# Attention and a routed feed-forward on one core: the down projection in three fp32r passes, the weight splitting begun earlier, the first expert tile turned ahead of the gates

## The chip, the cores and the metric

One core of one Trainium2 chip runs the whole program. The metric is the device time of one execution in microseconds (us), the median of several runs. Engines are called PE (TensorE; PEld its weight loads), DVE (VectorE), ACT (ScalarE), POOL (GpSimd) and SP (SyncE, which here only issues DMAs, in the order of its program). L1034 is line 1034 of the kernel before.

## The reference

The input x is 8 x 1024 tokens of 256 numbers. The steps are these, all in float32:

```python
xn = layernorm(x)
q, k, v = xn @ Wq + bq, xn @ Wk + bk, xn @ Wv + bv      # 4 heads of 256
scores  = (qr . kr + qi . ki) / 16     # of the 4 heads of one token with each other
s       = softmax(scores) @ v, heads swapped, @ Wo + bo
gates   = sinkhorn((xn @ router_w.T + router_b) / temp)  # 3 rounds, 8 experts
top 2 gates of each token, normalised
all_out = (relu(xn @ wg[e]) * (xn @ wp[e])) @ wo[e]      # 256 -> 512 -> 256, expert e
ffn     = xn + sum over the 2 experts of gate * all_out
out     = x + s * silu(ffn)
```

## The kernel before

The kernel goes through these stages.

**Prologue.** SP loads x in 16 blocks of 512 tokens. DVE and ACT normalise it, PE turns it and multiplies it by the router's weights (lines 798 and 808), and SP stores the normalised x to `xn_d`. Beside it the gate and up weights of the 8 experts, 16 pieces of 128 x 1024, are loaded over parts of x that are no longer needed (`load_raw`, line 288), split on POOL into a rounded fp32r part and the rest (`halve`, lines 516 and 519), and both parts are stored to a scratch tensor `w_d` (`store_split`, line 295). The staging buffers are `WH` and `WL`, four pieces deep; the semaphores `s_wst` tell that the stores have landed. When the last stores have landed, DVE splits Wq and Wk into the same buffers (`split`, lines 1132 and 1133). PE folds Wv and Wo into one matrix M (lines 880 and 883, 18 steps), and the first Sinkhorn rounds run between these steps.

**Attention, first half.** `segment(0, QE)` treats the blocks q = 0 to 3. For each there are 24 steps c: with c under 16 a chunk of q or k in three fp32r passes (high by high, high by low, low by high; L952), moved out of PSUM by ACT (L702) and DVE (L1447); with c from 16 on the values (L963), moved by ACT into `UN`, which holds three, and stored by SP (`write_u`, L331). Then 4 score steps follow (L909) with a softmax on DVE. Other DVE work is placed behind certain steps (`side`): the rest of Sinkhorn, the top two, `ranks`. POOL builds one-hot lists (`marks`), and SP stores M to `m_d` before the first block (L325).

**Expert stage.** NM = 135 tiles of 128 gathered tokens. Per tile m, PE runs in this order: `gt(m+1)` (2 transposes, L999), `up(m)` (12 fp32r matmuls of 512 columns with the split gate and up weights, L1017), `ht(m-1)` (4 transposes of the hidden tile, L1026), `down(m-2)` (4 plain fp32 matmuls of 256 columns, L1034; each leaves two records in the trace). ACT moves the turned tokens (`gt`), the relu of the gate, the turned hidden tile (`ht`, L746) and the result (`ye`). DVE subtracts the rounded tokens from the exact ones (`xgl`, L1495) and multiplies relu by up (L1506). POOL gathers tokens and scatters results by indirect DMA. Three experts' weights lie in SBUF; `load_expert` fetches 4096 columns from `w_d` and 1024 from `wo`. Ahead of the stage PE turns the gates into each token's order (`weigh`, 16 matmuls, L939), DVE copies them (`GP`), and only then does `gt(0)` run.

**Attention, second half, and the end.** `segment(QE, NQ)` does the blocks 4 to 15, with the sums over experts, silu and the output beside it.

Of the kernel before, what the change touches and what calls it, by code (L numbers as in the profile page):

```python
# [5 lines left out]
F32 = mybir.dt.float32  # L6
F32R = mybir.dt.float32r
# [29 lines left out]
def program(nc, x, phase, Wq, bq, Wk, bk, Wv, bv, Wo, bo, rw, rb, temp, wg, wp, wo, out):  # L37
# [8 lines left out]
    with ctx:  # L46
# [8 lines left out]
        w_d = nc.dram_tensor("w_d", [E * 128, 4096], F32).ap()  # L55
# [28 lines left out]
        TM = sb("TM", [128, 512])  # L84
        AB = sb("AB", [128, 2, 512])
# [12 lines left out]
        HT = AB[:, :, :].rearrange("p a (c n) -> p a c n", c=4)  # L98
# [96 lines left out]
        s_wst = [sem(f"s_wst{i}") for i in range(4)]  # L195
        s_xb, s_xt, s_xtc, s_xtd = sem("s_xb"), sem("s_xt"), sem("s_xtc"), sem("s_xtd")
# [36 lines left out]
        def raw(i):  # L233

            q = i + 1 if i < 2 * E - 1 else 5
            return WM[:, 1024 * q:1024 * q + 1024], s_x[q], 64 if i < 2 * E - 1 else 80
# [4 lines left out]
        def place_e(x):  # L241

            return 16384 - 5120 * (x % 3)
# [29 lines left out]
        def _(e):  # L273
            for q in range(NQ):
                e.dma_start(X[:, 4 * q:4 * q + 4, :], blk(xf, q)).then_inc(s_x[q], 16)
                if q == 3:
                    e.dma_start(Wv_s, Wv.rearrange("(k p) n -> p k n", p=128)).then_inc(s_wv, 16)
            for j in range(2):
                e.dma_start(Wo_s[j], Wo[512 * j:512 * j + 512, :].rearrange("(c p) n -> p c n", p=128)).then_inc(s_wo, 16)

            def load_raw(i):
                r, s, _ = raw(i)
                if i < 2 * E - 1:
                    e.wait_ge(s_x[i + 1], 48)
                    e.wait_ge(s_rt, 2 * i + 4)
                else:
                    e.wait_ge(s_wlo, 5)
# [3 lines left out]
            def store_split(i):  # L291
# [5 lines left out]
                if i < 4:  # L297
                    w, k = i // 2, i % 2
# [26 lines left out]
            e.dma_start(m_d, WM[:, 16384:24576]).then_inc(s_md, 16)  # L325
# [1206 lines left out]
```

## Time and profile before

| | us |
|---|---|
| median of 3 runs | 1757.52 (1756.17 to 1758.42) |
| the profiled execution's own time | 1760.04 |
| its span, first to last instruction | 1758.1 |
| expert stage, about | 386 to 1084 |
| first attention step | 136.01 |

PE is busy for 96% of the span, and most of the chain of work that ended last is on it. The times of a row are counted from the start of the span. The stage borders are read off the timeline, by the first L952 and the first L1017.

### The profile page before, as it was taken

The numbers are of one execution on the slowest core, as the hardware profiler recorded it, in microseconds if no ns is written. First come the engines' busy times: TensorE is split into PE (matmuls) and PEld (weight loads), VectorE is DVE, ScalarE is ACT, GpSimd is POOL, SyncE is SP. The second block draws the span as 40 slices with busy tenths as digits, with TensorE's granted clock in tenths as the row PEclk, the third lists the DMA queues.
The fourth block names the chain that finished last, engine by engine and source line by source line (L and its number), as shares of the span: only waits on it lengthen the run. The fifth ranks groups of instructions, "written<-read, shape, count | busy, mean of one in ns | idle before, by whom it ended". The sixth has DMA issues, their size and how long they took to land.

```text
span 1758.1 us, 26690 instructions
## 1 busy us (share of the span) xinstructions
PE 1683.1 (96%) x8788; PEld 1280.2 (73%) x8788; DVE 974.2 (55%) x1760; ACT 793.5 (45%) x1207; POOL 744.7 (42%) x865
## 2 busy tenths in 40 slices
PE   5889899999999999999999999999999999999994
PEld 2436766778888888888888888766877767877673
DVE  6567889962222222222222223778777788777785
ACT  4657335513333333333333335367564665644661
POOL 1671178713343333333343433343634645343435
PEclk9989899989999999999999999999999999999997
DMA  9984132172223131313111412424556345554234
GB/s 325 389 341 152 55 120 73 66 258 75 83 80 111 52 111 54 109 55 110 53 52 52 147 52 90 156 97 150 175 180 203 109 156 176 171 180 164 89 120 132
DMA packets 157085, 234.05 MB, mean 133 GB/s; under 512 B 13480, under 2 KB 120800, under 8 KB 155808
## 3 DMA queue, kind: packets, MB, share of 16 engines
q1 hardware_dynamic: 143488, 196.79, 32.7%
q0 software_dynamic: 12960, 35.41, 6.1%
q8 instruction: 81, 1.33, 0.3%
q14 instruction: 44, 0.36, 0.1%
q10 hardware_dynamic: 512, 0.16, 0.0%
HBM read 141.19 MB, written 91.11 MB: 132 GB/s over the span
## 4 chain that ended last, share of the span: by engine, by line
PE 83%; DVE 8%; DMA 3%; SPq 2%; ACT 2%; POOL 1%; issue 1%; ACTq 0%; POOLq 0%; DVEq 0%
PE ps L1017 21%; PE ps L952 17%; PE ps L1034 13%; PE ps L909 11%; PE ps L963 10%; PE ps L1026 3%; DMA WM<-in_L_ffn_wo_dram 2%; PE ps L921 2%; DVE WM L1447 2%; PE ps L999 2%; PE ps L808 1%; DVE UN L1097 1%; ACT WM L702 1%; PE ps L798 1%; DVE US L1381 1%
## 5 line engine op out<-in xcount | busy, mean ns | idle before, releaser
L1017 PE MATMUL ps<-WR,FR 128*128 x1620 | 407.5, 400 | 1.3 <-issue 0.7
L1017 PEld LDWEIGHTS ps<-WR,FR 128*128 128x128 f32 x1620 | 295.9, 189 | 58.7 <-issue 2.2
L702 ACT ACTIVATE WM<-ps,bcs,trig 128x512 f32<-128x512 f32 x256 | 314.0, 1261 | 35.2 <-PE ps L952 20.0
L1447 DVE TENSOR_SCALAR WM<-ps,vec,trig 128x512 f32<-128x512 f32 x256 | 290.1, 1186 | 35.6 <-ACT WM L702 34.8
L546 POOL DMA_INDIRECT y_d<-AUX x135 | 133.7, 990 | 390.6 <-ACT AUX L752 390.6
L1506 DVE TENSOR_TENSOR AUX<-AUX,ps 128x512 f32<-128x512 f32 x135 | 92.9, 688 | 340.6 <-ACT AUX L740 340.6
L1034 PE MATMUL ps<-WM,AB 128*128 x1080 | 255.5, 379 | 0.0
L909 PEld LDWEIGHTS ps<-WM 128*128 128x128 f32 x2048 | 232.2, 193 | 10.5 <-issue 5.8
L909 PE MATMUL ps<-WM 128*128 128x128 f32 x2048 | 236.3, 277 | 3.4 <-DVE TM L1343 3.4
L963 PE MATMUL ps<-WM,XTJ 128*128 128x512 f32 x512 | 237.2, 600 | 0.1
L740 ACT ACTIVATE AUX<-ps 128x512 f32<-128x512 f32 x135 | 80.6, 597 | 316.0 <-PE ps L1017 299.5
L952 PE MATMUL ps<-XH,WH 128*128 128x512 f32 x512 | 205.6, 402 | 4.7 <-issue 3.8
L1034 PEld LDWEIGHTS ps<-WM,AB 128*128 128x128 f32 x1080 | 194.7, 190 | 20.9
L952 PE MATMUL ps<-XH,WL 128*128 128x512 f32 x512 | 200.6, 392 | 0.0
L952 PE MATMUL ps<-XL,WH 128*128 128x512 f32 x512 | 200.6, 392 | 0.0
L1495 DVE TENSOR_TENSOR FR<-ps,FR 128x256 fp32r<-128x256 f32 x135 | 57.3, 425 | 205.3 <-ACT FR L733 205.2
L542 POOL DMA_INDIRECT AUX<-xn_d,AUX x135 | 132.0, 978 | 81.4 <-issue 40.1
L963 PEld LDWEIGHTS ps<-WM,XTJ 128*128 128x128 f32 x512 | 91.6, 190 | 96.9 <-issue 91.8
L558 POOL TENSOR_TENSOR AUX<-AUX,GP 128x256 f32<-128x256 f32 x120 | 77.3, 680 | 162.5 <-DMA AUX<-in_L_attn_x_dram 159.5
L709 ACT ACTIVATE UN<-ps 128x512 f32<-128x512 f32 x128 | 76.3, 596 | 133.6 <-PE ps L963 133.4
L719 ACT ACTIVATE SE<-SS 128x16 f32<-128x16 f32 x64 | 13.8, 216 | 236.6 <-DVE SS L1349 236.5
L752 ACT ACTIVATE AUX<-ps 128x256 f32<-128x256 f32 x135 | 52.0, 385 | 145.9 <-PE ps L1034 145.9
(225 smaller groups left out, 2081.5 us busy)
## 6 DMA issues: line engine op xcount, KB each, us to landing
u_d<-UN SPq DMA_DIRECT2D x128, 256.0 KB, 2.0
US<-u_d SPq DMA_DIRECT2D x64, 512.0 KB, 4.8
WR<-w_d SPq DMA_DIRECT2D x8, 2048.0 KB
AUX<-y_d SPq DMA_DIRECT2D x30, 512.0 KB, 5.8
WM<-in_L_attn_x_dram SPq DMA_DIRECT2D x16, 512.0 KB, 9.4
xn_d<-WM SPq DMA_DIRECT2D x32, 256.0 KB, 6.3
w_d<-WH SPq DMA_DIRECT2D x16, 512.0 KB, 6.4
w_d<-WL SPq DMA_DIRECT2D x16, 512.0 KB, 7.0
```

Source lines behind the costliest of these rows:

```text
L542: e.indirect_dma_start(XG[:, m % 2, :], None, xn_d, bass.IndirectOffsetOnAxis(gidx[:, m:m + 1], 0)).then_inc(s_g[m % 2], 16)
L546: e.indirect_dma_start(y_d, bass.IndirectOffsetOnAxis(toks[:, m - 5:m - 4], 0), YS[:, (m - 5) % 2, :], None).then_inc(s_y[(m - 5) % 2], 16)
L558: ins = e.tensor_tensor(y[:, i, :], y[:, i, :], GP[:, i, k, q, None].broadcast_to([128, D]), ALU.mult)
L702: e.activation(QT[:, 2 * x, i % 2, :].rearrange("p (t h) -> p t h", h=H)[:, :, i // 2], b, ACT.Identity, bias=bcs[:, x, 0, i:i + 1], scale ...
L740: e.activation(GR[:, :], mG[m % 2][:, :], ACT.Relu).then_inc(s_gr, 1)
L909: mm = e.matmul(pS[n % 2][:, 128 * c:128 * c + 128], QT[:, x, h, col:col + 128], QT[:, 2 + x, h, col:col + 128], start=(x == h == 0), stop ...
L952: mm = e.matmul(b[:, :], w[:, k, 128 * c:128 * c + 128], xx[:, k, :], start=(k == 0 and w is WH and xx is XH), stop=(k == 1 and w is WL))
L963: mm = e.matmul(b[:, :], XTJ[:, k, a // 2, :], M_s[:, k, 512 * a:512 * a + 512], start=(k == 0), stop=(k == 1))
L1017: mm = e.matmul(b[:, :], x, WR[:, bass.ds(off[m] + (2048 * z + 1024 * a + 512 * k), 512)], start=(k == 0 and x is xh and z == 0), stop=(k ...
L1034: mm = e.matmul(mY[m % 2][:, 0:256], HT[:, m % 2, c, :], WM[:, bass.ds(off[m] + (4096 + 256 * c), 256)], start=(c == 0), stop=(c == 3))
L1447: e.tensor_scalar(QT[:, 2 * x + 1, i % 2, :].rearrange("p (t h) -> p t h", h=H)[:, :, i // 2], ps[bank(24 * q + c)][:, :], bqk[:, x, i:i + ...
L1506: e.tensor_tensor(HS[:, m % 2, :], GR[:, :], mP[m % 2][:, :], ALU.mult).then_inc(s_h, 1)
```

## The change

**Down projection.** `wo` is split too, in 16 halves of 128 x 512. POOL does this after `xtj(0)` (`halve_down`: a copy that rounds, a subtraction, 128 x 512 each), in two buffers that take turns. SP loads each half (256 KB), waits for the split (`s_ho`), stores both parts (512 KB) to `w_d`, which grows to 6144 columns, and loads the next half but one. Eleven of these `store_half` steps stand ahead of the first `write_u` of block 0, the other five between its first `write_u`s. `ranks` on DVE and `load_expert` wait for these stores. The store of M to `m_d` moves behind block 1's first loads. `down` becomes 12 fp32r matmuls of 256 columns. The turned hidden tile is rounded by ACT into `HTH`; DVE gets a subtraction per tile, `htl`, 128 x 512 out of PSUM, behind its multiplication; the next `ht` waits for it (`s_htl`) instead of for ACT. An expert's load is one DMA of 6144 columns.

**Splitting of gate and up.** Five pieces have buffers of their own (three in `US`, two beyond Wv), and are loaded between x's blocks 1 to 6; the other eleven follow over x as before, from the fourth block stored on. `store_split` begins after the second block stored instead of after the fifth round of splits. The load of Wv moves behind x. ACT waits for five splits before it fills `WvT`.

**Gates.** `weigh` goes out of the segment; PE now does `gt(0)` first, then `weigh`, and DVE copies the gates after `xgl(0)`.

```diff
-            for q in range(NQ + 5):
+            for q in range(NQ):
+                e.dma_start(X[:, 4 * q:4 * q + 4, :], blk(xf, q)).then_inc(s_x[q], 16)
+                if 1 <= q <= 5:
+                    load_raw(q - 1)
...
+            for q in range(NQ + 1):
...
-                if 3 <= q < 3 + 2 * E:
-                    load_raw(q - 3)
-                if q >= 5:
-                    store_split(q - 5)
+                if 3 <= q < 2 * E - 2:
+                    load_raw(q + 2)
+                if q >= 1:
+                    store_split(q - 1)
...
+            def store_half(i):
+                e.wait_ge(s_ho, i + 1)
+                d = w_d[64 * (i - i % 2):64 * (i - i % 2) + 128, 4096:6144].rearrange("p (z f) -> p z f", z=2)
+                e.dma_start(d[:, :, 512 * (i % 2):512 * (i % 2) + 512],
+                            part[i % 2][1].bitcast(F32)).then_inc(s_hs[i % 2], 16)
+                if i + 2 < 2 * E:
+                    load_half(i + 2)
...
+                    if q == 0:
+                        load_half(0)
+                        load_half(1)
+                        for i in range(2 * E - 5):
+                            store_half(i)
+                    if q == 1:
+                        e.dma_start(m_d, WM[:, 16384:24576]).then_inc(s_md, 16)
                     for c in range(8):
                         write_u(q, c)
+                        if q == 0 and c < 5:
+                            store_half(2 * E - 5 + c)
...
+            def halve_down(i):
+                r, hl = part[i % 2]
+                e.wait_ge(s_hr[i % 2], 16 * (i // 2 + 1))
+                if i >= 2:
+                    e.wait_ge(s_hs[i % 2], 16 * (i // 2))
+                ch(e.tensor_copy(hl[:, 0, :], r))
+                e.tensor_tensor(hl[:, 1, :], r, hl[:, 0, :].bitcast(F32), ALU.subtract).then_inc(s_ho, 1)
...
                 for c in range(4):
-                    mm = e.matmul(mY[m % 2][:, 0:256], HT[:, m % 2, c, :],
-                                  WM[:, bass.ds(off[m] + (4096 + 256 * c), 256)], start=(c == 0), stop=(c == 3))
+                    hh, hl = HTH[:, m % 2, c, :], HTL[:, m % 2, c, :]
+                    for x, z in ((hh, 0), (hh, 1), (hl, 0)):
+                        mm = e.matmul(mY[m % 2][:, 0:256], x, WR[:, bass.ds(off[m] + (4096 + 1024 * z + 256 * c), 256)],
+                                      start=(c == 0 and x is hh and z == 0), stop=(c == 3 and x is hl))
...
+            e.wait_ge(s_sm1, 4 * QE - 1)
+            gt(0)
+            weigh()
             e.wait_ge(s_sm1, 4 * QE)
             e.wait_ge(s_gp, 2)
             e.wait_ge(s_ca, 24 * QE)
-            gt(0)
...
             xgl(0)
+            e.wait_ge(s_gp, 1)
+            e.tensor_copy(GP[:, :, :, :].rearrange("p i k q -> p (i k q)"), pD[:, 0:128]).then_inc(s_gp, 1)
...
+                if m >= 1:
+                    htl(m - 1)
+            htl(NM - 1)
```

## Rows read from the trace of the kernel before

**Rows 1.** The page, part 1: busy time of each engine over the span.

```profile
PE 1683.1 (96%) x8788; PEld 1280.2 (73%) x8788; DVE 974.2 (55%) x1760; ACT 793.5 (45%) x1207; POOL 744.7 (42%) x865
```

**Rows 2.** Chain of work that ended last, one expert tile (start, us, what).

```profile
1002.54 2.76 PE ps L1017 x12
1005.30 0.44 PE ps L1026 x4
1005.74 1.73 PE ps L1034 x8
1007.46 0.22 PE ps L999 x2
```

**Rows 3.** Windows view: stretch, engines busy (instructions), granted clock, DMA share, GB/s.

```profile
1000.00:1030.00 30.00, 30.00 (x154) 25.40 (x153) 6.68 (x12) 10.48 (x24) 10.96 (x12) 1.00 0.15 49
```

**Rows 4.** The page, part 5: DVE's product of relu and up, 128 x 512.

```profile
L1506 DVE TENSOR_TENSOR AUX<-AUX,ps 128x512 f32<-128x512 f32 x135 | 92.9, 688 | 340.6 <-ACT AUX L740 340.6
```

**Rows 5.** The same chain: 32 records of fp32 scores; 96 fp32r matmuls of 512 columns.

```profile
254.62 3.64 PE ps L909 x32
...
1083.97 21.86 PE ps L952 x96
```

**Rows 6.** Groups of instructions by form, PE's weight loads: busy us, mean ns, idle before.

```profile
L1017 PEld LDWEIGHTS ps<-WR,FR 128*128 128x128 f32 x1620 | 295.9, 189 | 58.7 <-issue 2.2
L909 PEld LDWEIGHTS ps<-WM 128*128 128x128 f32 x2048 | 232.2, 193 | 10.5 <-issue 5.8 <-DVE TM L1343 3.8 <-ACT UN L709 0.8
```

**Rows 7.** Timeline of POOL: first piece's rounding and subtraction, the last piece's subtraction.

```profile
41.87 1.18 POOL L516 CAST WH<-WM 128x512 fp32r<-128x512 f32 x2 [38.17 <-DMA WM<-in_L_ffn_wg_dram]
43.13 2.50 POOL L519 TENSOR_TENSOR WL<-WM,WH 128x512 fp32r<-128x512 f32 x2
...
122.18 2.94 POOL L519 TENSOR_TENSOR WL<-WM,WH 128x512 fp32r<-128x512 f32 x2
```

**Rows 8.** Windows of 5 us in the prologue, columns as in rows 3.

```profile
15.00:20.00 5.00, 1.24 (x5) 0.85 (x6) 4.46 (x19) 1.85 (x5) 0.00 (x0) 1.00 1.10 348
...
115.00:120.00 5.00, 2.09 (x5) 0.57 (x3) 2.82 (x2) 1.19 (x2) 4.92 (x6) 1.00 0.99 383
120.00:125.00 5.00, 2.21 (x4) 1.18 (x5) 4.93 (x5) 0.00 (x0) 4.92 (x4) 0.62 0.57 231
125.00:130.00 5.00, 4.89 (x7) 1.72 (x7) 4.88 (x8) 2.51 (x3) 0.12 (x1) 0.50 0.52 210
```

**Rows 9.** Timelines of DVE and PE: first split of Wq, first attention matmul.

```profile
117.14 1.27 DVE L1132 CAST WH<-WM 128x1024 fp32r<-128x1024 f32 x1 [4.20 <-DMA w_d<-WL]
...
136.01 0.47 PE L952 MATMUL ps<-XH,WH 128*128 128x512 f32 x1 [0.83 <-issue]
```

**Rows 10.** DMA view: issues, KB each, median us to landing.

```profile
u_d<-UN SPq DMA_DIRECT2D x128, 256.0 KB, 2.0
US<-u_d SPq DMA_DIRECT2D x64, 512.0 KB, 4.8
...
w_d<-WH SPq DMA_DIRECT2D x16, 512.0 KB, 6.4
```

**Rows 11.** Timelines of SP, ACT, DVE and PE in block 0.

```profile
142.55 1.39 SPq L320 DMA_DIRECT2D XB<-xn_d  x2
...
170.38 0.59 ACT L639 ACTIVATE XH<-ps 128x512 fp32r<-128x512 f32 x1
...
175.63 0.69 DVE L1323 TENSOR_TENSOR XL<-ps,XH 128x512 fp32r<-128x512 f32 x1
178.15 1.52 DVE L1234 TENSOR_TENSOR AUX<-AUX,ioe 128x512 f32<-128x512 f32 x1
...
184.80 9.04 PE L909 MATMUL ps<-WM 128*128 128x128 f32 x64 [2.21 <-DVE TM L1343]
```

**Rows 12.** Timeline of PE before the expert stage.

```profile
377.74 4.28 PE L939 MATMUL ps<-AUX 128*128 128x32 f32 x32
...
385.72 5.37 PE L1017 MATMUL ps<-WR,FR 128*128 x12 [0.66 <-issue]
```

**Rows 13.** The chain: load of expert 0, its last part.

```profile
367.24 12.81 DMA WM<-in_L_ffn_wo_dram
```

More of the change, by code:

```diff
@@ L84, in program @@
         TM = sb("TM", [128, 512])
+        with nc.sbuf_tensor("ABR", [128, 2, 512], F32R) as ABR:
+            pass
         AB = sb("AB", [128, 2, 512])
@@ L97, in program @@
         HS = AUX[:, 1536:2560].rearrange("p (a f) -> p a f", a=2)
-        HT = AB[:, :, :].rearrange("p a (c n) -> p a c n", c=4)
+        HTH = ABR[:, :, :].rearrange("p a (c n) -> p a c n", c=4)
+        HTL = FR[:, 6144:7168].rearrange("p (a c n) -> p a c n", a=2, c=4)
+        part = ((AUX[:, 6144:6656], ABR[:, :, :]),
+                (AUX[:, 4608:5120], FR[:, 3072:4096].rearrange("p (z f) -> p z f", z=2)))
         YS = AUX[:, 2560:3072].rearrange("p (a d) -> p a d", a=2)
@@ L195, in program @@
         s_wst = [sem(f"s_wst{i}") for i in range(4)]
+        s_ri = [sem(f"s_ri{i}") for i in range(5)]
+        s_hr = [sem(f"s_hr{i}") for i in range(2)]
+        s_hs = [sem(f"s_hs{i}") for i in range(2)]
+        s_ho, s_htl = sem("s_ho"), sem("s_htl")
         s_xb, s_xt, s_xtc, s_xtd = sem("s_xb"), sem("s_xt"), sem("s_xtc"), sem("s_xtd")
@@ L273, in _ @@
         def _(e):
[L274 to L279, printed above, removed]
             def load_raw(i):
                 r, s, _ = raw(i)
[L283 to L287, printed above, removed]
+                if i >= 5:
+                    e.wait_ge(s_x[i - 4], 48)
+                    e.wait_ge(s_rt, 2 * i - 6)
                 e.dma_start(r.rearrange("p (k f) -> p k f", k=2),
@@ L425, in _ @@
                 e.wait_ge(s_wst[i], 128)
+            for i in range(2):
+                e.wait_ge(s_hs[i], 16 * E)
             e.wait_ge(s_md, 16)
@@ L524, in _ @@
             xtj(0)
+            for i in range(2 * E):
+                halve_down(i)
             xtj(1)
@@ L641, in _ @@
             xt(0, 0)
+            e.wait_ge(s_wlo, 5)
             for k in range(4):
@@ L745, in ht @@
                     e.wait_ge(s_dn, m - 1)
-                e.activation(HT[:, m % 2, :, :].rearrange("p c n -> p (c n)"), mH[:, :], ACT.Copy).then_inc(s_htc, 1)
+                e.activation(HTH[:, m % 2, :, :].rearrange("p c n -> p (c n)"), mH[:, :], ACT.Copy).then_inc(s_htc, 1)
             def ye(m):
@@ L980, in segment @@
                         place(lists.get((q, 24 + i), ()))
-                if q1 == QE:
-                    weigh()
-                else:
+                if q1 == NQ:
                     for i in range(4):
@@ L1302, in experts @@
                 ch(e.tensor_reduce(iom[:, :], em3, AX.X, ALU.add))
-                e.tensor_scalar(ewl, iom[:, :], 32.0, 32.0, ALU.mult, ALU.add)
+                e.tensor_scalar(ewl, iom[:, :], 16.0, 16.0, ALU.mult, ALU.add)
                 e.tensor_copy(tendi, tend)
@@ L1497, in xgl, with htl @@
                                 ALU.subtract).then_inc(s_xgl, 1)
+            def htl(m):
+                e.wait_ge(s_htc, m + 1)
+                e.tensor_tensor(HTL[:, m % 2, :, :].rearrange("p c n -> p (c n)"), mH[:, :],
+                                HTH[:, m % 2, :, :].rearrange("p c n -> p (c n)").bitcast(F32),
+                                ALU.subtract).then_inc(s_htl, 1)
             xgl(0)
+            e.wait_ge(s_gp, 1)
+            e.tensor_copy(GP[:, :, :, :].rearrange("p i k q -> p (i k q)"), pD[:, 0:128]).then_inc(s_gp, 1)
             for m in range(NM):
```

40 lines of the change are left out of this document (23 added, 17 removed).

## The prediction

> **What bounds the kernel now.** I read the page's busy times first: PE has 96% of the span [rows 1]. Then the chain of waits. In the expert stage it lies on PE alone, tile after tile. Its four lines (2.76 up, 0.44 turning, 1.73 down, 0.22 turning) make a tile of 5.15 us [rows 2]. The windows view shows PE busy for 30.00 of 30.00 us there at a granted clock of 1.00 (2.4 GHz), DVE 6.68, ACT 10.48, POOL 10.96, DMA share 0.15 [rows 3]. So in this stage each microsecond taken off PE comes off the time, 135 times over. The prologue is different. The DMA engines are full from early on (share 1.10 at 15 to 20 us, still 0.99 at 115 to 120) and half idle only at its end (0.57 and 0.52) [rows 8], where POOL does the last splits up to 125.1 [rows 7] and attention begins at 136.01 [rows 9]. In block 0 of attention DVE is what ends last: PE's scores wait 2.21 us for it and go on at 184.80 [rows 11].
>
> **Down in three passes: the main term.** Taken out: 8 records in 1.73 us, 216 ns each. Put in: 12 fp32r matmuls of 256 columns, each with its own weight load. No row shows this form, so I bound its pitch (start to start).
> - Array time: 96 fp32r matmuls of 512 columns took 21.86 us, 228 ns each [rows 5]. Half the columns give 114 ns if all of it shrinks with them.
> - If the part above an fp32 record (228 against 216, 12 ns) is fixed per instruction, it is (216 / 2) + 12 = 120, and 124 with 230 ns (2.76 / 12) [rows 2] and 14 to 16 ns fixed.
> - Weight load: the 32 records of scores have 128 columns in fp32, which is two passes of 128, the same array time as 256 columns in one pass, and each loads 128 x 128 weights. They took 3.64 us, 114 ns each [rows 5]. The transposes, which stream less, still took 110 (0.44 / 4) [rows 2]. So a full weight load fits into about 110 ns and sets the floor.
>
> The bounds are 110 and 124. The likeliest value lies by the fp32r rows with a fixed part: 118. Twelve make 1.42 us, 0.31 less than 1.73; by 135 tiles that is **42 us** (110: 1.32, 55 us; 124: 1.49, 32 us).
>
> The Trainium skill ("TensorE: Matmul & The Clock Gate", Back-to-back issue gap) gives an isolated gap of N / 2.4 + 2.5 ns, 109 ns for 256 columns. By that page the term would be 12 x 109 = 1.31 us, an estimate that saves 57 us. The fp32 record of 216 ns agrees with the page's formula for 512 columns; the fp32r rows at 228 to 230 do not, and I go by them.
>
> **What hides the rest of a tile's new work.** `htl` is a DVE operation of 128 x 512 out of PSUM like the product, 688 ns [rows 4]. DVE has 6.68 us of work in 30 us, so with 6 more operations it has some 11 and stays under 40% [rows 3]. For the order: the product of tile m ends about 1.4 us after `up(m)`, `htl(m-1)` follows it at 2.1 us, and its readers are `ht(m)` and `down(m-1)`, which come behind `up(m+1)`, 4.8 us after `up(m)`. About 2.5 us of cover remain; if it were gone, up to 0.7 us a tile would show. An expert's load grows by a fifth (3 MB for 2.5), but between two experts' loads there are many tiles and three buffers. I cost both at nothing.
>
> **Prologue.** The bytes stay the same and the queue was full, so early splits can't pull much forward. Three things move. In the last 10 us the DMA engines worked at 0.57 and 0.52; what they moved (231 x 5 + 210 x 5 = 2.2 MB) takes 5.7 us at 383 GB/s, so the last store lands about 4.5 us earlier. The wait of DVE's first split for a store (4.20 us [rows 9]) shrinks by some 1.3 us, as the pieces stored after it are 0.5 MB more. POOL ends earlier, as the last raw piece comes about 8 us sooner, and DVE's splits run beside an idle POOL. Against this: POOL's first four splits now run beside DVE's statistics, and x's blocks arrive behind up to 2.5 MB of weights. The wait of 4.20 us covers a delay of up to some 3 us. I take **4 us gained** (bounds 0 and 6), with attention beginning at 132.
>
> **Halves of wo in block 0.** SP comes free at 142.55 + 1.39 = 144 [rows 11], less 4: 140. Two loads of 256 KB land at about 143 (2.0 us for such a DMA [rows 10], behind XB). One half on POOL is half of a piece: (1.18 + 2.50) / 2 = 1.84 us, 2.1 beside a busy DVE [rows 7]. Then comes its round trip: the store is issued, the load of the next but one is queued behind it, both land. The landing was 2.0 us for 256 KB of store and 4.8 for 512 KB of load [rows 10]; in a light queue I take 3.5 for the pair. A parity's cycle is then 1.9 + 0.1 + 3.5 = 5.5 us for two halves, 2.75 a half, between 2.1 (POOL or DMA full: 786 KB at 383 GB/s is 2.05) and 3.5 (6.4 us landing, as in a full queue).
>
> Behind them in SP's queue stands every `write_u` of block 0. `UN` holds three, so ACT's steps c = 19 and 20 wait for `write_u` 0 and 1, which stand behind `store_half` 10 and 11. Half 11 is done at 146.8 + 5 x 5.5 = 174.3; `write_u(0,1)` lands at about 177, and ACT's copy of the next block (it follows step 20, before at 170.38) comes at about 178. DVE reads this copy before the top two (before at 175.63; less the 4 us gained it would be 171.6) [rows 11]. So DVE goes on at 179. The 8 us of DVE work behind it may be stretched by POOL: the row at 178.15 took 1.52 us where an operation of the same size took 0.69 [rows 11]. I add 2. PE's scores then go on at 189 or 190 instead of 184.8: **5 us lost** against before, the 4 of the prologue already counted in. With 2.1 us a half it is 2 us gained; with 3.5, 12 lost. The other stores end at about 189, ahead of `ranks`; the M store has the idle queue of block 1. These I cost at nothing.
>
> **Gates.** Before, `weigh` at 377.74 took 4.28 us, and `up(0)` came at 385.72 [rows 12]: 3.7 us of copy, turning and subtraction stood behind it. `gt(0)` and `xgl(0)` now lie beside `weigh`, and only the copy and `gt(1)` are left, which would give 2.5 us. But the first expert's load takes 12.81 us to 380.05 [rows 13] and grows by up to a fifth, to 382.6. I take **2 us gained** (0 to 3).
>
> **The sum.** -42 + 5 - 2 = -39. The profiled execution took 1760.04 us, its span 1758.1, the median of the runs 1757.52, 2.5 lower than the profiled one. So a profiled 1721 and a median of **1718.5 us**. The forecast's own range: 55 + 2 + 3 = 60 gained gives 1697.5, 32 gained and 12 lost gives 1737.5. Both ends together are unlikely; I take 1702 to 1735 for this case.
>
> **Rivals.**
> - *The halves hold up block 0 for longer.* SP waits in order, so 16 round trips in a row may take over 3.5 us each, or DVE may be slowed all along. It would cost some 17 us, with 1733 as the time. For it: landings of 6.4 us in the full queue. Against it: the queue is light after 145. 16%.
> - *The weight load shows on PE: slower than before.* The load's record is 189 ns long [rows 6]. If fp32r matmuls can't hide more than their own 107 ns of it, the pitch goes towards 190: 12 x 190 = 2.28 us, 0.55 more than 1.73, 74 us by 135. With +5 and -2 the time is 1835. It decides from a pitch of 144 ns on (1.73 / 12), or a little less with the block's loss. Against it: scores have records of 193 ns, but their loads overlap, as 2048 of them are busy for 232.2 us, 113 each [rows 6]. But those are fp32, and no fp32r row is shorter than 228 ns. 7%. The Trainium skill ("TensorE: Matmul & The Clock Gate", What overlaps and what doesn't) states that weight loads overlap with matmuls only when they use other row groups. By that rule load and stream would add up here and the change would be slower; the scores' rows speak against it for full tiles.
> - *The three passes bring nothing*, since some switch between operands keeps the pitch at about 144 ns. Then +5 - 2 remain: 1760. 5%.
> - *Everything at its better end*: the pitch at 110 ns and the halves covered, 1698 to 1700. 7%.
>
> The forecast has 65%. What of 1718.5 lies between 1700 and 1738 holds the forecast and most of the first rival, about 8 in 10. A difference under 0.2% (3.5 us) can't be told from no change. Faster by more: the forecast, the first and the last rival, 88%. Within: 3%. Slower by more: 9%.
>
> **What would show it.** The chain's lines for `down`: 12 records in 1.3 to 1.5 us, a tile of 4.8, PE still without idle time in the stage. A first L952 at about 132. In block 0, SP's stores of halves with a spacing near 2.75 us, ACT waiting for DMA behind its values, and scores that go on near 189. `up(0)` at 383 or so after what came before. Wrong would be: a tile over 5 us, idle PE behind `htl`, or attention that begins no earlier than 136.

## The result and the profile after

| | before | after |
|---|---|---|
| median (range) | 1757.97 (1756.17 to 1761.29) | 1744.91 (1743.30 to 1749.04) |
| ratio, 95% interval | | 0.9927 [0.9903, 0.9951] |
| span of the profiled execution | 1758.1 | 1747.3 |
| first attention matmul | 136.01 | 129.05 |
| scores of block 0 go on | 184.80 | 194.58 |
| `weigh` | 377.74 | 388.92 |
| first `up` | 385.72 | 394.36 |
| second half of attention begins | 1083.97 | 1072.13 |

The changed kernel is 13 us faster, a third of the 39 us that I had forecast, and 26 us later than the predicted 1718.5. Half of the table is as expected: attention begins earlier, block 0 gives that back and more, the gates give a little. The miss is in the expert stage. It has to save 135 times 0.30 us, 40 us, and saves 20: 698.2 us before, 677.8 after. The profiled execution of the changed kernel is the slowest of its four (1749.04 us), so its trace is some 4 us longer than the median.

The page's busy times and, from the chain of waits, one undisturbed tile of the kernel after (start, us, what) answer to [rows 1] and [rows 2]:

```profile
PE 1644.6 (94%) x9328; PEld 1274.2 (73%) x9328; DVE 1059.0 (61%) x1895; ACT 793.3 (45%) x1207; POOL 773.4 (44%) x897
```

```profile
1004.56 2.76 PE ps L1058 x12
1007.32 0.44 PE ps L1067 x4
1007.75 1.43 PE ps L1077 x12
1009.18 0.22 PE ps L1040 x2
```

`down` is now L1077. Twelve matmuls take 1.43 us, 119 ns each, and a tile 4.84 us instead of 5.14. So in an undisturbed tile the change does what it says. The windows view, with columns as in [rows 3], first for the same 30 us and then for 4 us with a disturbance:

```profile
1000.00:1030.00 30.00, 30.00 (x186) 26.50 (x185) 10.70 (x19) 10.68 (x25) 12.54 (x13) 1.00 0.16 54
737.00:741.00 4.00, 4.00 (x10) 3.13 (x11) 0.27 (x1) 0.00 (x0) 0.64 (x1) 0.50 0.10 33
```

In the first there is nothing but PE's own work at full clock; the second shows a granted clock of 0.50. What led to it is seen in PE's waits (releaser; us in total, times, longest) and in the chain around it. L1040 is the turning of the gathered tokens (`gt`), L1058 `up`.

```profile
PE ps L1040 <- DMA AUX<-xn_d,AUX: 8.4, 5, 3.1
...
PE ps L1058 <- issue: 3.2, 5, 0.8
```

```profile
721.47 1.44 PE ps L1077 x12
...
724.89 10.77 DMA AUX<-xn_d,AUX
735.66 0.04 issue
735.71 0.69 PE ps L1040 x2
736.40 0.41 issue
736.81 5.13 PE ps L1058 x12
...
742.37 1.43 PE ps L1077 x12
```

A gather of 128 tokens, 128 KB, takes 10.77 us to land; away from a load the same gather lands 2.8 us after its issue (issued at 478.57, last landing record at 481.39). PE stands still for 3.1 us. Then its two transposes take 0.69 us for 0.22, 0.41 us pass in "issue", and `up` takes 5.13 us for 2.76, at the granted clock of 0.50. From `down` at 721.47 to the one three tiles on at 742.37 it is 20.90 us, where three tiles take 14.52. There are five such places, each where the load of an expert's weights runs:

| `down` to the third after it | us | over 14.52 | gather lands after |
|---|---|---|---|
| 479.99 to 496.86 | 16.87 | 2.35 | 8.56 |
| 554.94 to 572.33 | 17.39 | 2.87 | 9.24 |
| 635.25 to 653.69 | 18.44 | 3.92 | 8.61 |
| 721.47 to 742.37 | 20.90 | 6.38 | 10.77 |
| 805.30 to 823.81 | 18.51 | 3.99 | 8.55 |

That makes 19.5 us, nearly all of the 20 that are missing in the stage. The timeline around the first place, first SP's queue and then POOL's (start, us, instruction, idle before and its releaser):

```profile
481.45 0.32 SPq L451 DMA_DIRECT2D WR<-w_d  x1
```

```profile
482.11 0.99 POOL L588 DMA_INDIRECT y_d<-AUX  x1 [2.58 <-ACT AUX L795]
483.41 0.97 POOL L584 DMA_INDIRECT AUX<-xn_d,AUX  x1 [0.30 <-issue]
```

The load of 3 MB is issued 2.0 us ahead of the gather. The two loads whose landing the chain shows (issued at 392.51 and 402.92) took 10.4 and 10.5 us. At the five places the trace's DMA records end the load's data 10.1 to 12.0 us after its issue, and the gather lands 0.4 to 0.7 us after that. Without a delay the transposes would come some 7.5 us after the gather's issue. The kernel before had the same neighbourhood (load issued at 477.76), and PE never waited in it. Its POOL and PE:

```profile
479.73 0.97 POOL L542 DMA_INDIRECT AUX<-xn_d,AUX  x1 [0.30 <-issue]
```

```profile
487.85 0.38 PE L999 MATMUL ps<-ident,AUX 128*128 128x128 f32 x2
```

There the transposes came 8.1 us after the issue, and the gather had landed. The load was of another form: two DMAs, 2 MB in rows of 16 KB and 512 KB of `wo` in rows of 1 KB, where the changed kernel has one of 3 MB in rows of 24 KB.

**Block 0.** SP's queue shows the halves' stores (L345) and the values' stores (L354, `write_u`); the store at 173.05 is ten halves after the first:

```profile
141.66 0.37 SPq L345 DMA_DIRECT2D w_d<-ABR  x1
...
173.05 0.37 SPq L345 DMA_DIRECT2D w_d<-ABR  x1
...
173.97 0.87 SPq L354 DMA_DIRECT2D u_d<-UN  x1
175.84 0.37 SPq L345 DMA_DIRECT2D w_d<-FR  x1
...
176.77 0.47 SPq L354 DMA_DIRECT2D u_d<-UN  x1
```

The spacing is (173.05 - 141.66) / 10 = 3.1 us. What follows is in the chain and in DVE's timeline:

```profile
176.77 4.26 DMA u_d<-UN
...
194.58 9.04 PE ps L952 x64
```

```profile
165.79 1.60 DVE L1278 TENSOR_TENSOR AUX<-AUX 128x512 f32<-128x512 f32 x1
...
182.30 0.69 DVE L1369 TENSOR_TENSOR XL<-ps,XH 128x512 fp32r<-128x512 f32 x1 [11.09 <-ACT XH L681]
...
189.46 1.17 DVE L1297 TENSOR_TENSOR AUX<-AUX 128x64 f32<-128x64 f32 x1
```

The second `write_u` lands only after 4.26 us, DVE has been idle for 11.09 us and goes on at 182.30 (before at 175.63), and needs 12.3 us to the scores where it had needed 9.2. The short operation shown, 128 x 64, took 1.17 us, and an operation of 128 x 512 ahead of the wait 1.60; what they take without the halves is seen below. In [rows 11] the scores went on at 184.80.

**The ends.** PE's timeline at the start of attention and at the gates answers to [rows 9] and [rows 12]:

```profile
129.05 0.47 PE L995 MATMUL ps<-XH,WH 128*128 128x512 f32 x1 [0.83 <-issue]
...
388.92 3.66 PE L982 MATMUL ps<-AUX 128*128 128x32 f32 x32
...
394.36 5.48 PE L1058 MATMUL ps<-WR,FR 128*128 x12 [0.88 <-DVE FR L1538]
```

From `weigh` to `up(0)` it is 5.4 us now and was 8.0. Of these 2.5 us, 0.6 are `weigh` itself (3.66 us for 4.28).

### The profile page after: what moved, and what is told of

The parts are those of the page before. It is cut to its first block, busy times and chain, and to the rows that moved or that the text cites. A ratio compares the mean times of both kernels' runs of the same rounds, so it can differ in the third digit from the quotient of the medians.

```text
span 1747.3 us, 28514 instructions
## 1 busy us (share of the span) xinstructions
PE 1644.6 (94%) x9328; PEld 1274.2 (73%) x9328; DVE 1059.0 (61%) x1895; ACT 793.3 (45%) x1207; POOL 773.4 (44%) x897
## 4 chain that ended last, share of the span: by engine, by line
PE 78%; DMA 9%; DVE 7%; POOL 3%; SPq 2%; issue 1%; ACT 1%; ACTq 0%; POOLq 0%; DVEq 0%
PE ps L1058 19%; PE ps L995 17%; PE ps L952 11%; PE ps L1006 11%; PE ps L1077 10%; PE ps L1067 3%; DMA AUX<-xn_d,AUX 3%; DMA WR<-w_d 2%; PE ps L964 2%; PE ps L1040 2%; DVE WM L1493 1%; DMA AUX<-in_L_ffn_wo_dram 1%; PE ps L851 1%; DVE UN L1142 1%; PE ps L907 1%
## 5 line engine op out<-in xcount | busy, mean ns | idle before, releaser
L1058 PE MATMUL ps<-WR,FR 128*128 x1620 | 413.1, 404 | 4.4 <-issue 3.2
L1058 PEld LDWEIGHTS ps<-WR,FR 128*128 128x128 f32 x1620 | 299.5, 192 | 64.9 <-issue 6.2
L1006 PE MATMUL ps<-WM,XTJ 128*128 128x512 f32 x512 | 239.0, 603 | 13.4 <-ACT UN L752 13.2
L1077 PE MATMUL ps<-WR,ABR 128*128 x1080 | 209.4, 292 | 0.0
L1077 PEld LDWEIGHTS ps<-WR,ABR 128*128 128x128 f32 x1080 | 165.5, 190 | 0.0
L1077 PE MATMUL ps<-WR,FR 128*128 x540 | 152.0, 281 | 0.0
L537 POOL TENSOR_SCALAR OH<-AUX 128x128 bf16<-128x128 f32 x96 | 88.4, 932 | 65.9 <-DVE AUX L1336 36.4
```

The lines of the kernel that those rows point to most:

```text
L537: e.tensor_scalar(rank1h[:, j % 16, :], ior_f, slot_p[:, k, n:n + 1], mark[:, k, n:n + 1], ALU.is_equal, ALU.mult).then_inc(s_oa, 1)
L1006: mm = e.matmul(b[:, :], XTJ[:, k, a // 2, :], M_s[:, k, 512 * a:512 * a + 512], start=(k == 0), stop=(k == 1))
L1058: mm = e.matmul(b[:, :], x, WR[:, bass.ds(off[m] + (2048 * z + 1024 * a + 512 * k), 512)], start=(k == 0 and x is xh and z == 0), stop=(k ...
L1077: mm = e.matmul(mY[m % 2][:, 0:256], x, WR[:, bass.ds(off[m] + (4096 + 1024 * z + 256 * c), 256)], start=(c == 0 and x is hh and z == 0), ...
```

## Experiments

All are edits of the changed kernel, and each was timed beside runs of the kernel before on the same chip. They ran on three chips, and the kernel before had medians of 1756.0 to 1758.4 beside them, so differences of 2 or 3 us between medians of the table are read with the ratios' intervals. The theory is that the gather's landing behind an expert's load is what the expert stage lost, and that the halves in SP's queue are what block 0 lost.

| kernel | median | ratio to before, 95% |
|---|---|---|
| changed kernel | 1744.9 | 0.9927 [0.9903, 0.9951] |
| four gather buffers | 1742.9 | 0.9914 [0.9898, 0.9931] |
| load in six DMAs | 1724.2 | 0.9811 [0.9795, 0.9828] |
| no halves | 1715.3 | 0.9764 [0.9748, 0.9780] |
| six halves ahead | 1732.5 | 0.9859 [0.9841, 0.9877] |
| six halves ahead and six DMAs | 1712.4 | 0.9747 [0.9726, 0.9768] |
| four buffers, scatter later | 1722.9 | 0.9798 [0.9782, 0.9814] |
| the combination, splitting late | 1719.9 | 0.9777 [0.9760, 0.9793] |
| the combination, gates as before | 1715.3 | 0.9754 [0.9738, 0.9770] |
| load in two DMAs | 1730.5 | 0.9846 [0.9821, 0.9870] |
| the combination, four halves earlier | 1715.5 | 0.9751 [0.9725, 0.9777] |
| `down` as before | 1748.6 | 0.9945 [0.9930, 0.9961] |
| load smaller by a sixth | 1732.0 | 0.9862 [0.9842, 0.9882] |

**Four gather buffers.** If the gather comes late, let it be issued earlier.

```diff
-        XG = AUX[:, 0:512].rearrange("p (a d) -> p a d", a=2)
+        XG = [AUX[:, o:o + 256] for o in (0, 256, 5120, 5376)]
...
-                    if m >= 2:
-                        e.wait_ge(s_gt, m - 1)
+                    if m >= 4:
+                        e.wait_ge(s_gt, m - 3)
...
```

> The changed kernel with four buffers for gathered tokens, so that each gather is issued one tile (4.84 us) earlier. Theory 1: the expert stage loses some 20 us because a gather that is issued while an expert's 3 MB load runs lands only with it (8.6 to 10.8 us), while its transpose comes 7.6 us behind the issue; one more tile of slack covers that. Then PE's idle time for gathered tokens (17.8 us) goes, no half-clock stretches follow, and the time falls by 15 to 20 us against the changed kernel (1725 to 1730). Rival: PE waits for the expert's weights themselves or for DVE's new subtraction; then the idle time keeps its places and the time stays at 1745 within 2 us.

Measured 1742.9, only 2 us less, with intervals that overlap: a miss. (The 17.8 us of idle time named there count PE and its weight loads each; PE's own waits for a gather were 8.4 us.) POOL's and PE's timelines of this kernel say why:

```profile
482.60 0.97 POOL L584 DMA_INDIRECT AUX<-xn_d,AUX  x1 [0.30 <-issue]
```

```profile
491.61 0.44 PE L1040 MATMUL ps<-ident,AUX 128*128 128x128 f32 x2 [1.33 <-DMA AUX<-xn_d,AUX]
```

The gather is issued no earlier. On POOL it stands behind the scatter of an older tile, and this waits for ACT's result (`s_ye`). The buffers were not what held it. The edit did not test the theory; it showed that I had looked at one of two waits.

**The expert's load in six DMAs.** The same 3 MB, but in rows of 4 KB instead of 24 KB.

```diff
-                e.dma_start(WR[:, b:b + 6144].bitcast(F32), w_d[128 * x:128 * x + 128, :]).then_inc(s_wl, 16)
+                for j in range(6):
+                    e.dma_start(WR[:, b + 1024 * j:b + 1024 * j + 1024].bitcast(F32),
+                                w_d[128 * x:128 * x + 128, 1024 * j:1024 * j + 1024]).then_inc(s_wl, 16)
...
```

> The changed kernel with each expert's load cut into six DMAs of 1024 columns (rows of 4 KB instead of 24 KB), same bytes. Theory 1a: the DMA engines take rows of the two queues in turns, so a gather of 1 KB rows passes a load of small rows quickly: gathers land in 2 to 4 us, the stalls go, 1725 to 1730. Theory 1b: what is queued first goes first, whatever the row size: gathers still land with the load, and the time stays at 1743 to 1746. Rival (PE waits for the weights themselves): same or a little slower.

Measured 1724.2, 20.7 us less than the changed kernel. No wait for a gather is left among PE's waits, and the "issue" ahead of `up` (now L1060) is down from five times to once:

```profile
PE ps L1060 <- issue: 0.7, 1, 0.7
```

The 20.7 us match the 19.5 of the table of stalls; measured in the same way, the five loads of this kernel cost 1.0 us together. The volume is the same, so the volume alone does not explain the late gather.

**Four buffers and the scatter one tile later.** Now the gather is issued one tile earlier, with the load as in the changed kernel. The first buffer edit is kept; added is:

```diff
-                if m >= 5:
-                    e.wait_ge(s_ye, m - 4)
+                if m >= 6:
+                    e.wait_ge(s_ye, m - 5)
...
```

> The changed kernel with four buffers for gathered tokens, and the scatter of a tile's result put one place later in POOL's order, behind the next gather. With four buffers alone a gather still stood behind the scatter of tile m-6 and was issued 7.5 us ahead of its transpose, as before; now it stands behind that of tile m-7. The theory (slack against a landing of 8.6 to 10.8 us) expects the distance to grow to some 12 us, no idle time of PE for gathered tokens, and 1725 to 1728 us with the load's rows of 24 KB left as they are. If landing with the load is not what PE waits for, the time stays at 1743.

Measured 1722.9, with no wait for a gather. POOL's and PE's timelines:

```profile
479.53 0.97 POOL L584 DMA_INDIRECT AUX<-xn_d,AUX  x1 [0.31 <-issue]
```

```profile
491.90 0.27 PE L1040 MATMUL ps<-ident,AUX 128*128 128x128 f32 x1
```

There are 12.4 us between issue and use instead of 7.5. Two unlike edits, one on the load and one on the gather, give the same 21 to 22 us back. That the stalls were the gather's is settled by this.

**The load in two DMAs.** Rows of 12 KB, to see whether the landing follows the length of a row.

```diff
-                e.dma_start(WR[:, b:b + 6144].bitcast(F32), w_d[128 * x:128 * x + 128, :]).then_inc(s_wl, 16)
+                for j in range(2):
+                    e.dma_start(WR[:, b + 3072 * j:b + 3072 * j + 3072].bitcast(F32),
+                                w_d[128 * x:128 * x + 128, 3072 * j:3072 * j + 3072]).then_inc(s_wl, 16)
...
```

> The changed kernel with each expert's load in two DMAs of 3072 columns (rows of 12 KB), same bytes. If the DMA engines take rows of the two queues in turns, a gather of 128 rows of 1 KB gets through when eight rows of the load have gone by on each engine: with 24 KB rows that is the whole load (8.6 us), with 12 KB rows half of it, some 5 us, which the distance of 7.5 us covers: stalls gone, 1724 to 1727. If the landing doesn't go with the row but 4 KB rows helped for another reason (more DMAs, issued over a longer time), the time lies between, 1730 to 1740.

Measured 1730.5. POOL's and PE's timelines:

```profile
478.72 0.97 POOL L586 DMA_INDIRECT AUX<-xn_d,AUX  x1 [0.30 <-issue]
```

```profile
486.63 0.44 PE L1042 MATMUL ps<-ident,AUX 128*128 128x128 f32 x2 [0.23 <-DMA AUX<-xn_d,AUX]
487.77 3.01 PE L1060 MATMUL ps<-WR,FR 128*128 x12 [0.70 <-DMA WR<-w_d]
```

The gather landed about 7.8 us after its issue, and I had expected 5. Half the row did not halve the landing. The length of the rows matters, but not in proportion. The DMA records of the traces show a part that does not go with it: with a load running, the first packet of POOL's queue starts 4.3 to 4.7 us after the issue of the scatter ahead of the gather with rows of 24 and of 12 KB, and 3.0 to 4.6 with rows of 4 KB; without a load it starts 1.56 us after it. The five loads of this kernel cost 6.7 us, about 1.3 each, though the gather is only 0.3 to 0.4 us late. The profile names the load as what ended the wait of `up`; but `up` waits for the weights of its own tile's expert, which had landed long before, on a semaphore that all loads share.

The Trainium skill ("DMA: Bandwidth & Descriptors", Queues, rings and completion order) says that each DMA engine goes round between the queues that have work, and changes over only after a whole packet. That longer rows of the load keep a gather waiting is in line with it. Whether the queues took turns in this way, and how long a turn was, no row here shows.

**The load smaller by a sixth.** Is it the growth of the load that did it, or the shorter tile, which moves the transposes from 8.1 to 7.5 us behind the gather's issue? The edit takes 5120 columns again in one DMA, and reads the rounded down weights twice, so it leaves their low part out. It shortens the rows too, from 24 to 20 KB.

```diff
-                e.dma_start(WR[:, b:b + 6144].bitcast(F32), w_d[128 * x:128 * x + 128, :]).then_inc(s_wl, 16)
+                e.dma_start(WR[:, b:b + 5120].bitcast(F32), w_d[128 * x:128 * x + 128, 0:5120]).then_inc(s_wl, 16)
...
```

> The changed kernel with one thing taken back: an expert's load is 5120 columns again (2.5 MB, 20 KB a row, one DMA) instead of 6144. The second pass of the down matmul reads the rounded weights a second time instead of the low part, so the low part of the down weights is left out of the computation; the number of matmuls, their sizes and the halves written in block 0 stay. Theory (the gather's rows queue beside the load's, and lose because the load now lasts longer than the time in which the gather is wanted): the load takes 8.7 to 9.6 us instead of 10.4, the gather behind it lands 6.8 to 7.8 us after its issue instead of 8.6 to 10.8, and transposes want it after 7.5, so the five stalls of 2.4 to 6.4 us go or shrink to under 1 us each; time 1725 to 1730 us. Rival (the shorter tile alone moves the transposes up to the gather, whatever the load's size): the gather still lands after 8 us or more, stalls of 2 us and more remain, time 1740 us or more.

Measured 1732.0, between what the two expect. Two pieces of this kernel's chain, at the first load and at the fourth:

```profile
481.17 7.79 DMA AUX<-xn_d,AUX
...
489.01 0.44 PE ps L1040 x2
489.44 0.67 issue
...
725.20 1.42 PE ps L1077 x12
726.62 0.44 PE ps L1040 x2
727.06 0.67 issue
```

The gather now lands after 7.79, 8.31 and 8.84 us at the first three loads, and in time at the others. Measured like the stalls of the changed kernel, the five cost 1.28, 1.78, 2.34, 1.17 and 1.15 us, 7.7 in all. So of the 19.5 us some 12 (12.9 by the medians, 11.4 by the ratios to before) came with the step from 20 KB and 2.5 MB to 24 KB and 3 MB, and 7.7 are there with 2.5 MB. It fits that 1724.2 + 7.7 is 1731.9. At the distance of the kernel before, 8.1 us, two of these three gathers would still have been late, so the shorter tile alone is not what makes them late either.

What is left is the form of the load. All kernels of this table have the tile of 4.84 us, and the cost is measured like that of the stalls above:

| load of an expert | MB | transposes after the gather's issue, us | cost of the five loads, us |
|---|---|---|---|
| one DMA, rows of 24 KB (changed kernel) | 3 | 8.9 to 10.8 | 19.5 |
| one DMA, rows of 20 KB | 2.5 | 7.7 to 8.9 | 7.7 |
| two DMAs, rows of 12 KB | 3 | 7.8 to 7.9 | 6.7 |
| two DMAs, rows of 16 and 8 KB (next kernel) | 3 | 7.5 to 7.9 | 3.9 |
| six DMAs, rows of 4 KB | 3 | 7.5 | 1.0 |

With the same 3 MB the cost goes from 19.5 down to 1.0 us. So the fifth more of bytes is not by itself what hurt, but that it came together with the step from two DMAs to one with longer rows. Whether the length of a row or the number of DMAs does it was not separated, and the form of the kernel before at the new pace was not run. In the trace of before the landings on record for the gathers behind these loads end 6.8 to 7.4 us after the issue (some records are missing), which is inside the 7.5 us too.

**No halves.** `load_half`, `store_half` and `halve_down` are taken out, and the load fetches 2048 columns of gate and up a second time in place of the down weights.

```diff
-                        load_half(0)
-                        load_half(1)
-                        for i in range(2 * E - 5):
-                            store_half(i)
...
```

> The changed kernel without the splitting of the down weights: no loads, splits and stores of halves in block 0. The down weights are left out, and the expert's load takes 2048 of the gate and up columns a second time in their place (3 MB as before, in two DMAs of 16 and 8 KB rows). Theory 2: the halves cost block 0 of attention 17 us, as write_u stands behind eleven of them in SP's queue; without them the scores of block 0 go on 15 to 17 us earlier (at 178 instead of 194.6) and the time falls by as much, to 1728 to 1730, apart from what two smaller DMAs change in the expert stage. Rival: block 0 is slow because attention began early and DVE's Sinkhorn work is as long as ever; then no more than 5 us are gained.

Measured 1715.3, below the 1728 to 1730 expected. The chain has the scores at 177.29, 17 us earlier than in the changed kernel:

```profile
177.29 7.41 PE ps L931 x64
```

DVE's timeline of this kernel, the same step as at 189.46 in the changed one, and ahead of them the operation whose 1.52 us I had read as stretched:

```profile
170.65 1.52 DVE L1258 TENSOR_TENSOR AUX<-AUX,ioe 128x512 f32<-128x512 f32 x1
...
175.22 0.21 DVE L1276 TENSOR_TENSOR AUX<-AUX 128x64 f32<-128x64 f32 x1
```

The long operation takes 1.52 us without the halves too, the short one 0.21 us instead of 1.17, and its neighbour 0.20 for 1.04. Long ones are not spared either: the operation that took 1.60 us at 165.79 in the changed kernel takes 0.69 here (at 164.51). From DVE's subtraction to the scores it is 9.2 us here (168.14 to 177.29), as before the change.

The load is two DMAs here, of 4096 and 2048 columns, so most of the gather's stalls are gone too (3.9 us are left of 19.5, see the table above); the price of the halves is read from the scores and from the next two kernels, and not from this time.

**Six halves ahead.** Six instead of eleven `store_half` steps stand ahead of the first `write_u`, eight follow one by one behind the `write_u`s, two come after them.

```diff
-                        for i in range(2 * E - 5):
+                        for i in range(6):
                             store_half(i)
...
-                        if q == 0 and c < 5:
-                            store_half(2 * E - 5 + c)
+                        if q == 0:
+                            store_half(6 + c)
```

> The changed kernel with six instead of eleven halves ahead of block 0's first write_u, then one half behind each of the eight, and the last two behind them. The same work, another place in SP's queue. Theory 2a (queue order): half 5 is issued near 158 instead of half 10 at 173, so ACT's values wait little and DVE goes on near 171 instead of 182; 9 to 12 us gained, 1733 to 1736. Theory 2b (POOL beside DVE and traffic slow block 0 whatever the order): under 4 us gained.

Measured 1732.5, 12.4 us less. DVE's timeline and the chain of this kernel:

```profile
172.65 0.69 DVE L1372 TENSOR_TENSOR XL<-ps,XH 128x512 fp32r<-128x512 f32 x1
```

```profile
181.43 9.04 PE ps L955 x64
```

DVE's subtraction is at 172.65 instead of 182.30, with no wait of 11 us ahead of it, and the scores are 13.2 us earlier. Six kernels with eleven halves ahead have these scores at 193 to 195.5, and the three with six ahead and the early splitting at 181.43, 182.47 and 185.34. So the order in SP's queue was the main loss, and what the halves still cost with the new order is the difference to 177.29, 4 to 8 us.

**Both together.** Six halves ahead, and the load in six DMAs.

> The changed kernel with both cures: six halves ahead of the first write_u, and the expert's load in six DMAs of 1024 columns. The two losses lie in different stages, so the gains should add: 20.7 and 12.4 us under 1744.9, some 1712 us. If the row size acted on block 0 too, or the cures share a cause, the sum would be smaller by 5 us or more (1717 and up).

Measured 1712.4, ratio 0.9747 [0.9726, 0.9768]: the fastest of all, 46 us below the kernel before and 32.5 below the changed one. The two gains (12.4 and 20.7) add up to 33.1. In its expert stage PE's waits amount to half a microsecond:

```profile
PE ps L1063 <- issue: 0.3, 1, 0.3
PE ps L1072 <- DVE FR L1549: 0.2, 1, 0.2
```

**Four halves earlier.** The combination with four halves split on POOL ahead of `xtj(0)`, in the prologue's last microseconds, and only four more ahead of the first `write_u`.

```diff
...
+            for i in range(4):
+                halve_down(i)
             xtj(0)
-            for i in range(2 * E):
+            for i in range(4, 2 * E):
                 halve_down(i)
...
```

> The kernel with both cures, and with the first four halves split by POOL before xtj(0), loaded and stored while DMA engines and POOL are idle (115 to 128 us), four more ahead of the first write_u. Theory: the halves end 8 to 10 us earlier and run less beside DVE's top-two work, so scores of block 0 go on 2 to 4 us earlier: 1708 to 1711. Rival: SP and POOL are held by the early halves while M's last steps wait for them (brow, XB, xtj), and block 0 begins its values later: 1713 to 1718.

Measured 1715.5, no gain. The time is the rival's, but its reason isn't shown: the chain's scores came at much the same point as in the combination (182.47), and took longer, with a granted clock of 0.50 from 182 to 186:

```profile
181.99 10.10 PE ps L962 x64
```

**The combination with the splitting of before, and with the gates of before.** Each undoes one of the other two parts of the change.

```diff
-            if i < 3:
-                return US[:, i, :, :].rearrange("p c d -> p (c d)"), s_ri[i], 16
-            if i < 5:
-                return WM[:, 15360 + 1024 * i:16384 + 1024 * i], s_ri[i], 16
-            return WM[:, 1024 * (i - 4):1024 * (i - 3)], s_x[i - 4], 64
+            q = i + 1 if i < 2 * E - 1 else 5
+            return WM[:, 1024 * q:1024 * q + 1024], s_x[q], 64 if i < 2 * E - 1 else 80
...
```

> The kernel with both cures, but with the splitting of gate and up in the order and at the time of the kernel before (raw pieces over x, first load behind the fourth block stored, Wv between x's blocks). Measures the early splitting alone. From the traces: attention begins 7 us later (136 instead of 129), and the time is 5 to 7 us longer, 1717 to 1719. Rival: block 0 waits for DVE and the halves anyway and swallows it; then under 2 us.

```diff
-            gt(0)
-            weigh()
             e.wait_ge(s_sm1, 4 * QE)
             e.wait_ge(s_gp, 2)
             e.wait_ge(s_ca, 24 * QE)
+            gt(0)
...
```

> The kernel with both cures, but weigh in its old place and gt(0) behind the copy of the gates. Measures the third part alone: 1.5 to 3 us longer (1713.5 to 1715), with up(0) beginning 8.0 instead of 5.4 us behind the first instruction of weigh. Rival: the load of expert 0 lets up(0) begin no earlier either way; then the two are equal.

By the medians the early splitting is worth 7.5 us (1719.9 against 1712.4; the intervals of the ratios overlap between 0.976 and 0.977). PE's first attention matmul is 2.6 us later than the combination's 130.91, and about 4 later than in most kernels with the early splitting (128.5 to 129.9), but 2.5 us earlier than the kernel before with the same splitting has it (136.01):

```profile
133.47 0.47 PE L997 MATMUL ps<-XH,WH 128*128 128x512 f32 x1 [0.83 <-issue]
```

The spans differ by 8.5 us. Of these, 2.6 lie ahead of attention, 3.4 between its start and `weigh`, and 2.5 behind. The stretch from the start of attention to `weigh` takes 243.0, 245.9 and 249.4 us in three kernels that have the same order of halves and the same splitting (the combination, six halves ahead, gates as before). So the 2.6 to 4 us ahead of attention can be put down to the splitting, and the rest is not shown. For the gates PE's timeline shows 7.1 us from `weigh` to `up(0)` (8.0 expected), and 5.4 in the combination, so 1.7; the medians differ by 3, with overlapping intervals.

```profile
379.08 3.66 PE L987 MATMUL ps<-AUX 128*128 128x32 f32 x32
...
386.19 5.48 PE L1065 MATMUL ps<-WR,FR 128*128 x12 [0.79 <-issue]
```

**`down` as before.** The other two parts alone, with fp32 `down`, no halves and 5120 columns.

> The changed kernel with the down projection as before (plain fp32, wo loaded from its own tensor, no halves, no htl, 5120 columns): the early splitting and the gates alone. From the traces: attention begins 5 to 7 us earlier, up(0) 2 us nearer to weigh; 1748 to 1751. Then the down part, as it was built, brought only 4 to 6 us of the 13 that the change gained. Rival: the two parts are worth less alone, as DVE holds block 0: 1754 and up.

Measured 1748.6. So the main part of the change, as built, brought 3.7 us by the medians, which is not clear of noise (0.9945 [0.9930, 0.9961] against 0.9927 [0.9903, 0.9951]), of the 40 that PE's work shrank by: 19.5 went to the stalls, and the scores of block 0, which this kernel has at 179.71, went on 14.9 us later.

## Why the prediction was wrong

The direction was right, and two of the sum's three terms hold, `down` and the gates. The time was wrong by 26 us, and outside the range. In the spans (1719 worked out, 1747.3 measured) the difference is 28 us:

| term | forecast | trace | difference |
|---|---|---|---|
| `down`, 135 tiles | -42 | -40.5 | +1.5 |
| stalls behind an expert's load | 0 | +19.5 | +19.5 |
| block 0, prologue counted in | +5 | +9.8 | +4.8 |
| blocks 1 to 3 | 0 | +1.4 | +1.4 |
| gates | -2 | -2.5 | -0.5 |
| second half, and the rest of the stage | 0 | about +1.6 | +1.6 |

**The pitch** was to be 118 ns by the fp32r rows with a fixed part per instruction, and is 119. The rows were the better guide than the 109 of the formula in the Trainium skill ("TensorE: Matmul & The Clock Gate", Back-to-back issue gap). The rival of weight loads that show on PE is refuted: the loads' records are still longer than the pitch, and they overlap. The Trainium skill's rule ("TensorE: Matmul & The Clock Gate", What overlaps and what doesn't) does not hold for these full 128 x 128 tiles. The rival in which the passes bring nothing fell with it. The cover for `htl` held: an undisturbed tile takes 4.84 us, with PE busy in all of it.

**The failed step** is this one: "An expert's load grows by a fifth (3 MB for 2.5), but between two experts' loads there are many tiles and three buffers. I cost both at nothing." The load cost 19.5 us, in five stalls of 2.4 to 6.4 us. I asked only whether the weights would come in time, and they did: PE's waits show 0.2 us for them, once. I did not ask what shares the DMA engines with the load while it runs. The gather behind it is needed by a fixed time. A faster tile asks for it sooner (7.5 us after its issue instead of 8.1), and the new load lets it land later (8.6 to 10.8 us), less by its fifth of bytes than by its form, one DMA with rows of 24 KB; my working named only the bytes. The load itself lasts hardly longer: 10.4 us, and before 9.9 (380.13 to 390.02). The trace of before held the warning. Its gather was issued 8.1 us before its use, beside a load of 9.9 us, where away from a load it lands in 2.8, and no row said how much of the 8.1 was free. That PE was busy in 30.00 of 30.00 us came from a stretch without a load. The windows view would have to be read where a load runs as well, and the distance of each transfer's issue from its use set beside the load's length.

**A late gather costs more than its wait.** The waits add up to 8.4 us, the stalls to 19.5. At each the transposes took 0.44 or 0.69 us for 0.22, 0.4 to 0.8 us of issue came ahead of `up`, and in three of the five `up` took 4.6 to 5.1 us for 2.76, at a granted clock of 0.50 to 0.61. My sum would have been too low even with the wait in it.

**Block 0** had the right mechanism and terms that were too small. SP's queue did hold up the values' stores. Half 1 was stored at 144.05, where the working has it done at 146.8, but with 3.1 us a half for my 2.75 half 11 came at 175.84 instead of 174.3. Then `write_u` took 4.26 us to land for my 2.0, a median over light and full queues alike, and DVE went on at 182.3 for my 179. From there I had 8 us and 2 for a stretch; it took 12.3, and the 8 was too short from the start: before, it was 9.2 (175.63 to 184.80). That gives 194.6 for 189, although attention began 3 us before my 132. The stretch was also read from the wrong row: the 1.52 us in [rows 11] is what that operation takes without the halves too, and what grew in this stretch were operations of 128 x 64, from 0.2 to over 1 us. The rival in which the halves hold block 0 for longer is true in part: counted from the start of attention 16.7 us went, near its 17, but against before only 9.8. Its time of 1733 does not follow from its terms (1757.5 - 42 + 17 - 2 is 1730.5), and the hold-up without the stalls gave 1724.2.

**The prologue** gave 7.0 us in this trace for my 4, and 5 to 7.5 in those of the other kernels with this prologue, around the better bound of 6. But the kernel with the splitting of before has 133.47, so not all of it is shown to be the splitting's. The DMA engines work at a share of 1.05 in the windows view until 120 and have nothing left to do at 125, where before they worked at half until 130 [rows 8]; POOL's last split is done before that too. The granted clock is 1.00 from 115 to 130, where before it was 0.62 and 0.50 from 120 on [rows 8]; what this gave was not measured. **The gates** came to 2.5 us for my 2, of which the kernel with the gates as before shows 1.7.

## What to carry to other kernels

Before a large load beside a loop is made larger, or its rows longer, or the loop faster, take every small transfer that is issued while the load runs, and compare its distance from issue to use with the load's whole length: the small one may land only with the large one. Splitting the large load into DMAs with shorter rows, or issuing the small one a step earlier past everything that it stands behind, costs little and gave 21 us here. In a queue that works in order, put no series of round trips ahead of a store that frees a buffer: one between each two such stores moved the same work at 12 us less.

## What had not been expected of the hardware

- A gather of 128 KB on POOL's queue, issued 2 us behind a load of 3 MB with rows of 24 KB, took 8.6 to 10.8 us, as long as the load. With rows of 12 KB it took 7.8; with 4 KB it was in time for a use 7.5 us after the issue. Away from a load it landed 2.8 us after the issue.
- Where PE's semaphore came late, the restart cost 1.15 us even with next to no wait: in the kernel with the smaller load, at the fourth and fifth load, the transposes took 0.44 us for 0.22, and 0.67 us of issue stood ahead of `up`, with no wait shown ahead of the transposes. The instructions ahead of `up` read two registers and wait on a semaphore by a register's value; that PE's sequencer normally runs these ahead of the engine, and loses that lead, is argued and was not tested.
- After a stall of 3.1 us the granted clock was 0.50, and `up` took 5.13 us for 2.76.
- In block 0, with POOL at the halves and the DMA engines full (share 1.02 at 180 to 185), DVE's operations of 128 x 64 took 1.0 to 1.2 us instead of 0.2, and those of 128 x 512 took 1.64 for 1.52 us there, but earlier in the block, also beside the halves, 1.60 for 0.69. Whether POOL or the DMAs slow them was not separated.
